# Gated cross-attention block with routed experts: other places for the row stores and for three steps at a batch's end

## The reference

```
x = x + tanh(g_xattn) * attention(layernorm(x), ctx, ctx)      # softmax(Q K^T / sqrt(8)) V, 16 heads, then Wo
n = layernorm(x);  xn = rms_norm(n) * norm_scale
scores = xn @ w_router.T                                        # 8 experts, best two by score
h = val * silu(gate)                                            # per expert, 352 wide
x = x + tanh(g_ffn) * (sum over two of probs * (h @ w_down) + n)
```

## Time and profile before

| | us |
|---|---|
| median of three runs | 449.42 (448.97 to 450.76) |
| the profiled execution's own time | 447.54 |
| its span, first to last instruction | 445.7 |
| PE busy | 402.6 (90%) |
| DVE busy | 302.0 (68%) |
| ACT busy | 260.9 (59%) |
| POOL busy | 242.5 (54%) |

### The profile page before, as it was taken

One profiled execution on the slowest core, in us unless ns is written; L12 is line 12 of the kernel. 1 busy time (PEld: TensorE's weight loads), 2 busy tenths in 40 slices (PEclk: granted clock), 3 DMA queues, 4 the chain that ended last, 5 costly groups with the idle time before them and its releaser, 6 DMA issues.

```text
span 445.7 us, 13323 instructions
## 1 busy us (share of the span) xinstructions
PE 402.6 (90%) x3821; PEld 272.8 (61%) x3824; DVE 302.0 (68%) x1167; ACT 260.9 (59%) x582; POOL 242.5 (54%) x201
## 2 busy tenths in 40 slices
PE   8989889999899888898888899899899999999991
PEld 3536455655556545555565468677578777787771
DVE  5878788887887787878787555466755555555550
ACT  3527487777777768675766456653445555555540
POOL 7082232244655545544433438868787448876664
PEclk9998999999889899998985699999999999999997
DMA  7625151545658724224101224444545334444320
GB/s 193 171 59 133 33 132 38 134 128 160 147 154 213 193 62 116 75 62 121 57 23 45 59 75 72 88 57 86 86 74 73 50 46 57 59 60 59 33 24 0
DMA packets 57422, 39.07 MB, mean 88 GB/s; under 512 B 8819, under 2 KB 55158, under 8 KB 57366
## 3 DMA queue, kind: packets, MB, share of 16 engines
q1 hardware_dynamic: 43622, 28.87, 25.4%
q0 software_dynamic: 12736, 8.64, 14.0%
q10 hardware_dynamic: 1008, 0.85, 0.8%
HBM read 14.26 MB, written 11.75 MB: 58 GB/s over the span
## 4 chain that ended last, share of the span: by engine, by line
PE 66%; DVE 16%; issue 7%; ACT 6%; DMA 2%; SPq 1%; POOLq 0%; another core or an unknown queue 0%; POOL 0%; DVEq 0%; ACTq 0%
PE bank L1595 12%; PE bank L1573 10%; PE bank L1575 10%; DVE nmx L840 5%; PE bank L1585 5%; PE bank L1361 5%; PE bank L1388 3%; PE bank L1393 3%; PE bank L1335 2%; ACT pt L573 2%; PE bank L1348 2%; PE bank L1303 2%; PE bank L1565 2%; PE bank L1304 2%; PE bank L1399 1%
## 5 line engine op out<-in xcount | busy, mean ns | idle before, releaser
L509 POOL DMA_INDIRECT out<-ys,yi x72 | 112.0, 1556 | 45.0 <-issue 24.6
L427 POOL DMA_INDIRECT slots_dram<-xr,slu x64 | 63.1, 985 | 68.0 <-ACT pt L573 55.3
L840 DVE TENSOR_REDUCE nmx<-bank 128x4 f32<-128x512 f32 x128 | 81.9, 681 | 6.5 <-PE bank L1335 6.2
L573 ACT ACTIVATE pt<-bank 128x512 f32<-128x512 f32 x128 | 72.4, 594 | 14.8 <-PE bank L1348 9.1
L1595 PEld LDWEIGHTS bank<-wf_sb,hT 128*128 128x128 f32 (+1 forms) x432 | 56.3, 190 | 25.1 <-issue 21.3
L1193 DVE TENSOR_TENSOR hh<-sg,bank 128x352 f32<-128x352 f32 x72 | 37.4, 521 | 50.0 <-ACT sg L707 25.4
L1595 PE MATMUL bank<-wf_sb,hT 128*128 (+1 forms) x432 | 61.8, 279 | 5.2 <-DVE hT L1203 3.7
L715 ACT ACTIVATE ys<-bank,yc 128x128 f32<-128x128 f32 x72 | 26.5, 368 | 62.3 <-PE bank L1595 31.2
L1361 PE MATMUL bank<-pt,v 128*9 128x128 f32 x1024 | 52.4, 290 | 5.5 <-ACT pt L573 4.9
L1573 PE MATMUL bank<-wf_sb,xT 128*128 x144 | 55.7, 469 | 0.2
L1575 PE MATMUL bank<-wf_sb,xT 128*128 x144 | 54.5, 460 | 0.0
(11 more groups left out here) (191 smaller groups left out, 696.7 us busy)
## 6 DMA issues: line engine op xcount, KB each, us to landing
qs<-parts SPq DMA_DIRECT2D x48, 128.0 KB
ks<-parts SPq DMA_DIRECT2D x45, 128.0 KB
xs<-slots_dram SPq DMA_DIRECT2D x72, 66.0 KB
wf_sb<-in_wup SPq DMA_DIRECT2D x8, 352.0 KB
x_sb<-in_x SPq DMA_DIRECT2D x8, 256.0 KB, 3.6
ctx_sb<-in_ctx_in SPq DMA_DIRECT2D x8, 256.0 KB, 3.6
out<-x_sb SPq DMA_DIRECT2D x8, 256.0 KB
out<-ys,yi POOLq DMA_INDIRECT x72
```

The lines of the kernel that those rows point to most:

```text
L427: nc.gpsimd.indirect_dma_start(out=slots_dram, out_offset=bass.IndirectOffsetOnAxis(ap=slu[:, c % 2, k, kk:kk + 1], axis=0), in_=xr[:, c % ...
L509: nc.gpsimd.indirect_dma_start(out=out.rearrange("b s d -> (b s) d"), out_offset=bass.IndirectOffsetOnAxis(ap=yi[:, r:r + 1], axis=0), in_ ...
L573: nc.scalar.activation(pt[:, 4 * g:4 * g + 4, :], STB[g % 2][:, :].rearrange("p (h s) -> p h s", h=4), ACT.Exp, scale=SCORE_SCALE).then_in ...
L840: nc.vector.tensor_reduce(nmx[:, b % 2, at:at + 4], SB[g % 2][:, :].rearrange("p (h s) -> p h s", h=4), AX.X, ALU.max, negate=True).then_i ...
```

## The change

On POOL, the row stores are placed one by one. A store called early waits for `d_mT` of b + 2 or more, that is until the previous iteration's maximum is copied; one called late waits for `a_aT` of b or more, the copied attention of batch b - 1 in this iteration. Each batch of the loop still has two, but the sets are shifted by one: set 5 (early) and 6 (late) at u = 0, 7 and 0 at u = 1, 1 and 2 at u = 2, 3 and 4 at u = 3. At u = 0, 1 and 2 the early one stands ahead of `low`, `power2` and `rotate_k`. Behind the loop three stores follow without a wait, where there were two. On PE, the list at the end of an iteration becomes weighted values 2, `project_out(b - 1)`, `transpose_maximum(b + 2)`, weighted values 3. On DVE, `add_attention`, `widen` and `statistics1` go ahead of `maximum_high` and `maximum_low`.

```diff
--- before.py
+++ after.py
@@ -428,16 +428,15 @@
                     out=slots_dram, out_offset=bass.IndirectOffsetOnAxis(ap=slu[:, c % 2, k, kk:kk + 1], axis=0),
                     in_=xr[:, c % 2, k, kk, :], in_offset=None).then_inc(scattered[c % 2], 16)
 
-            def scatter_between(b, c, k):
-
-                for kk in range(2):
-                    pool.wait_ge(a_exp, 4 * b + 2 + 2 * kk)
-                    scatter(c, k, kk)
-
-            def scatter_both(c, k):
-
-                for kk in range(2):
-                    scatter(c, k, kk)
+            def scatter_early(b, c, j):
+
+                pool.wait_ge(d_mT, min(b + 2, B))
+                scatter(c, j // 2, j % 2)
+
+            def scatter_late(b, c, j):
+
+                pool.wait_ge(a_aT, b)
+                scatter(c, j // 2, j % 2)
 
             nc.gpsimd.memset(mhalf[:, :, :], -0.5).then_inc(zeroed, 1)
             nc.gpsimd.memset(ks[:, 0, :, :].bitcast(U32), 0x3F803F80).then_inc(zeroed, 1)
@@ -464,28 +463,36 @@
             for b in range(B):
                 c, u = b // CH, b % CH
                 if u == 0:
+                    if there(c - 3):
+                        scatter_early(b, c - 3, 5)
                     if there(c + 1):
                         low(c + 1, 1)
                     if there(c - 3):
-                        scatter_between(b, c - 3, 3)
+                        scatter_late(b, c - 3, 6)
                 if u == 1:
+                    if there(c - 3):
+                        scatter_early(b, c - 3, 7)
                     if there(c - 1):
                         power2(c - 1)
                     if there(c - 2):
-                        scatter_between(b, c - 2, 0)
+                        scatter_late(b, c - 2, 0)
                 if u == 2:
+                    if there(c - 2):
+                        scatter_early(b, c - 2, 1)
                     if there(c + 2):
                         rotate_k(c + 2)
                     if there(c - 2):
-                        scatter_between(b, c - 2, 1)
+                        scatter_late(b, c - 2, 2)
                 if u == 3:
                     if there(c - 2):
-                        scatter_between(b, c - 2, 2)
+                        scatter_early(b, c - 2, 3)
+                        scatter_late(b, c - 2, 4)
                     if there(c + 2):
                         low(c + 2, 0)
                     if there(c + 3):
                         power(c + 3)
-            scatter_both(NCH - 3, 3)
+            for j in range(5, 2 * CH):
+                scatter(NCH - 3, j // 2, j % 2)
             power2(NCH - 1)
 
             def send(q):
@@ -1145,6 +1152,12 @@
                     statistics(c + 3)
                 if u == 3 and there(c + 3):
                     variance(c + 3)
+                if real(b - 1):
+                    add_attention(b - 1)
+                if u == 3 and there(c + 3):
+                    widen(c + 3)
+                if real(b - 1):
+                    statistics1(b - 1)
                 if real(b + 2):
                     maximum_high(b + 2)
                     maximum_low(b + 2)
@@ -1165,12 +1178,6 @@
                     tiles_spread(0)
                 if b == CH * (NA + 2) + 2:
                     tiles_listed(0)
-                if real(b - 1):
-                    add_attention(b - 1)
-                if u == 3 and there(c + 3):
-                    widen(c + 3)
-                if real(b - 1):
-                    statistics1(b - 1)
                 if u == 0 and there(c - 1):
                     statistics2(c - 1)
                 if b == CH * (NA + 2) + 1:
@@ -1542,11 +1549,12 @@
                     list_tiles(0, b)
                 if real(b):
                     weighted_values(b, 2)
-                    weighted_values(b, 3)
+                if real(b - 1):
+                    project_out(b - 1)
                 if real(b + 2):
                     transpose_maximum(b + 2)
-                if real(b - 1):
-                    project_out(b - 1)
+                if real(b):
+                    weighted_values(b, 3)
 
 
             pe.wait_ge(d_tab, 1)
```

## The result

Measured side by side on one chip, the changed kernel took 455.22 us in the median of four runs (452.31 to 456.03) and the kernel before 450.09 (448.97 to 451.2). The ratio is 1.0106, 95% interval 1.0058 to 1.0155: slower by 1.1%, where the forecast was 446.6 and the range ended at 451.8.

A forecast was written before the change was run, and what follows sets the result against it. Bound: TensorE and VectorE waits in the batch loop, lengthened where TensorE's results are told late behind stores. Terms +0.6 (batches 1 to 7), 0 (8 to 11), -3.3 (12 to 23), -0.1 (24 to 31): -2.8, 446.6 us; range 442.3 to 451.8.

The forecast's parts named there:

- Batches 1 to 7: Batches with no stores: the later copy of the maximum costs 1.8 us, TensorE's reordering wins 1.2, together +0.6.
- the gain of 12 to 23: Three groups of four batches with stores: each group 28.78 to 27.7 us, -1.1 per group, -3.3 in all.
- "right": Signs: batches 12, 16, 20 near 6.7, 18 and 22 near 7.6; VectorE's pre-copy idle under 6, TensorE's copy wait 8+.
- "wrong": Signs against: results held with no store in the 1.7 us before, late copy releases, or batches 12 to 23 unchanged.
- the sign of the slower case: Maximum's copy released over 0.3 us behind the transpose's end in more than a third of the batches.
- The held results and the stores' places: TensorE results finishing 0.3 to 1.3 us after a store's start are told late; moved late stores cost 0.45 per group.
- placement is worth nothing: Rival: held results have another cause and stay, only the two orders act; about +2 us, 451.4; chance 0.14.
- TensorE's order: Batch tail: product first, fourth weighted values last; 0.49 us won in batch 4, 0.1 to 0.2 mostly, nothing at u = 3.
- VectorE's order: Sum and statistics before the maximum's copy; TensorE loses nothing at u = 0, 0.2 at u = 1 and 2, 0.5 at u = 3.
- SP's queue: SP issues the maxima rows up to 0.6 us later, a whole batch ahead of their scores; priced at nothing.
- The slower rival: L1335's second group at batch start: late stores delay the maximum's copy; 0.9 us per batch, nine hits 453.3; chance 0.16.

The follow-up runs named there:

- places_guarded: Kernel before with only the stores' new places, plus the last three stores waiting for the last copy of the weighted values: 442.87 us, ratio 0.9878.
- group 2: Follow-up session on a chip that does not hold results, kernel before 438.37 us; the changed kernel there took 448.07, ratio 1.0236.
- group 3: Follow-up session on a chip that holds results, kernel before 447.83 us; parts of the change were run, the changed kernel itself was not.
- widen_table_back: Changed kernel with the variances' small sum behind the maximum's copy and the tile table ahead of the residual sum again: 450.77 us, ratio 1.0058 to kernel before.
- before_again: Kernel before, unchanged, run once more with a profile on a chip that does not hold results: 438.98 us.
- after_again: Changed kernel, unchanged, run again on a chip that does not hold results: 448.07 us, ratio 1.0236 to the kernel before.

## Why the prediction was wrong

**The sum, term by term.** Between the two profiled executions the span grew by 7.5 us. Batches 1 to 7 gave +4.0 (forecast +0.6), 8 to 11 +0.1 (0), 12 to 23 -0.3 (-3.3); for 24 to 31 and what follows the forecast had -0.1 in all. Batches 24 to 30 gave -4.8, but there the mean granted clock was 0.79 before and 0.92 after, which is no merit of the change; from the start of batch 31 on it was +8.1. So three terms failed: the gain of 12 to 23 was eaten, batches 1 to 7 cost over six times as much, and the end was not priced. Of my signs, VectorE's idle time before the copy (0.4) and TensorE's wait for its second half (9.6) came out as for "right", since they name the wait and not its price. Batches 18 and 22 took 7.83 each (7.6). Batches 12, 16 and 20 were to be near 6.7 and take 7.55 at full clock, and batches 12 to 23 the same in sum (87.52 and 87.79) was one of the signs for "wrong". The copy's start was over 0.3 behind the transpose's end in 29 of 32 batches, but through VectorE's own queue and not by a late release, which is what the sign of the slower case asked for.

**The held results and the stores' places: right, on a chip that holds results.** A store starts, and TensorE's results are told late; moved, the stores strike fewer of them. places_guarded won 1.2% on such a chip, and batches 21 and 22 of the changed kernel took 5.78 and 7.83 (I had 5.9 and 7.6), the same as on chips that hold nothing. The rival "placement is worth nothing" is what a chip of the other kind gives, where the ratio was 1.001. It was luck, and not in the forecast, that the first measurement fell on a chip of the first kind. I had set the rule in the Trainium skill (SBUF — State Buffer, section "SBUF: two separate sides", that TensorE never waits on anyone) against rows 5 and 6. In four of five groups nothing speaks against it. In the others results come late behind the stores, but the rule is about SBUF's ports, and no run here shows whether a port is what delays them; what fails is my step from that rule to "the stores' places are worth nothing".

**TensorE's order: wrong in sign.** I took the pieces of batch 4 as if each kept its length in any order ("0.49 won", "where the exponent is no limit nothing is won"). From the third weighted values to the next batch the new order takes 1.46 nearly everywhere, which is 0.27 longer at u = 3. Batch 4 won 0.25 instead of 0.49 (5.36 with this order alone, 5.60 before), and at u = 3, where I had zero, it lost 0.32. For the kernel it is 0.5 to 1.1% lost where I had a small win.

**VectorE's order: the mechanism right, the size too small.** I had a cost of nothing at u = 0, 0.2 at u = 1 and 2 and 0.5 at u = 3, and against it 0.5 won at u = 0: 0.4 per group. Batches 12 to 15 took 28.76, 28.64 and 29.42 in the changed kernel on three chips that hold nothing (the last with batch 13 at a clock of 0.75), and 27.38 without VectorE's order: 1.3 at full clock. By place it is +0.64 at u = 0, -0.35 at u = 1, +0.4 to +0.7 at u = 2 and +0.39 at u = 3. I had argued that VectorE "comes out of u = 3 some 0.5 sooner"; it comes out later, because at u = 3 a third step went ahead of the copy, the sum of variances. It stands in the diff as widen, and no term of my sum had it. It ran 0.57 instead of 0.15 because GpSimd's low parts ran at the same time. With it back, u = 0 took 6.92 to 7.13 instead of 7.55, which is the length without VectorE's order (6.91), and still above my 6.7.

**Batches 1 to 7: the mechanism right, the sum small.** Predicted +0.6, measured 45.20 to 49.17, +4.0. The part "TensorE's order wins 1.2" came to nothing: with that order alone they took 45.93, with the stores' places alone, on the same chip, 46.07. The later copy, priced at 1.8, is nearly all of the 4.0: beside TensorE's order it took batch 3 from 6.87 to 7.44, batch 4 from 5.36 to 6.40 and batch 7 from 6.88 to 7.26.

**The end of the loop: not counted.** I had looked at the three unguarded stores for what stands behind them on GpSimd's queue, and not for what TensorE finishes beside them; and the tile table, a one-time step of VectorE, I had not followed past the residual sum. From the start of batch 31 on the change loses 8.1 us on the first chip and 1.45 in group 2. TensorE's start of the last heads by query is 3.8 later in time (258.63 and 254.83), while batch 31 began 0.68 sooner, so 4.5 of the 8.1 lie in that piece: 11.13 instead of 6.65. Other traces split it, as an estimate over chips. Without held results the changed kernel takes 8.76 there, at the same clock of 0.50, so some 2.4 are the hold by the unguarded stores (the 2.46 of the row above). The kernel before takes 7.40 there at a clock of 0.55, so 1.4 are the two orders, the table among them. The last 0.7 go with the clock, which was 0.74 in this piece of the first profile of the kernel before. In group 3 the piece took 10.51 with the four stores unguarded (widen_table_back) and 6.99 with the guard (places_guarded, which has neither order). The other 3.7 came up among the expert tiles, 2.0 of them between tiles 14 and 28 (38.44 instead of 36.42, at full clock in both). The changed kernel took 35.4 to 35.8 for these tiles on three other chips, so this is not shown to be the change's; its cause was not tried.

**SP's queue** I had priced at nothing. TensorE's wait for the stacked rows is 3.4 us, but it is 4.7 in before_again, so it can't be put down to the change.

**The slower rival named the right wait.** L1335's second group behind the maximum's copy, 1.4 per batch at worst, was its place. But I tied it to held results and asked for nine hits; it needs none. On the chips that hold nothing, the same wait is 9.2 and 9.0 us in two traces of the changed kernel, and the kernel 2.1 to 2.4% slower. That the time came out near this rival's 453.3 is luck, since its hits did not happen: in 30 of 32 batches the copy's delay in the first profile of the changed kernel is that of after_again, on a chip that holds nothing, within 0.02. I had the copy's delay worked out in batch 4 (0.49, with no store) and then let it be covered elsewhere by waits that the change itself removes.

**How the whole adds up.** Without held results: places 0.1%, TensorE's order 0.5 to 1.1%, VectorE's on top 1.2 to 1.6%, whole 2.1 to 2.4%. On the first chip the whole was 1.1%. The 1.0 to 1.3% between them is the size of what the places win on such a chip (1.2%), which fits the theory. It is inferred across chips and not shown, since the two orders without the places never ran on one that holds results. The places also regain only 5 of the 9 to 12 us that separate the two kinds of chip.

## What to carry to other kernels

Before pricing a step that moves ahead of another, follow what the other one releases, and on which engine: filling a hole in VectorE's queue ahead of a copy that TensorE waits for moves the hole to TensorE, which was 90% busy. The length of a matmul group belongs to its neighbours: count where weight loads were hidden and how many pairs of like groups the new order breaks. Take every step that the diff moves, small ones too, through the sum: at u = 0 it was the one without a term that cost. And a profile from one chip can carry a mechanism that another chip does not have, so run the kernel before on a second chip ahead of building a change on one.

## What the runs showed of the hardware

The same kernel took 448 to 450 us in the first measurement and in group 3, and 437.6 to 438.5 in the other four groups. In the traces one thing goes with it: whether what TensorE finishes within 1.3 us of the start of a GpSimd indirect store is told late (the 0.84 of rows 5 against 0.04; 88 of 161 results against none of 153). Why this happens on some chips, and whether it accounts for all of the difference, stays open.

VectorE's sum over 128x4 numbers took 0.15 us alone and 0.57 while GpSimd's operation on 128x512 numbers ran, to the end of that operation (87.29 + 1.16 = 88.45; the sum ended at 88.48). Over the changed kernel's eight such sums the median is 0.66, over the eight of widen_table_back 0.15.
